# Macaron block (MoE, attention, MoE) on one core: the routing of the second MoE's first half moved later into the last attention batches, with filler products on TensorE

## The reference, cut to what matters

```python
def ffn(x, gate_w, expert_bias, w1, w2, w3):      # 8 experts, top 2, hidden 352
    scores = softmax(x @ gate_w.T)
    _, sel = top_k(scores + expert_bias, 2)
    # token t goes to its two experts, scaled by its score BEFORE the expert
    routed = x[token_idx] * top_scores_sorted[:, None]
    out_rows = (silu(routed @ w1[e]) * (routed @ w3[e])) @ w2[e]   # e by row
    return zeros.at[token_idx].add(out_rows)

def attn(x, Wq, Wk, Wv, Wo):                      # 16 heads of width 8, no mask
    return softmax(q @ k.T / sqrt(8)) @ v @ Wo.T

x = hidden_states                                 # 16 x 256 tokens, width 128
x = x + 0.5 * ffn(layernorm(x), ...)
x = x + attn(layernorm(x), ...)
x = x + 0.5 * ffn(layernorm(x), ...)              # same weights again
```

## Time and profile before

| | us |
|---|---|
| median of 3 runs | 765.34 (761.83 to 770.02) |
| the profiled execution | 765.52 |
| its span | 763.7 |
| start to attention's batch 0 | 254.5 |
| batches 13, 14, 15 with the seam's first part | 469.08 to 529.46 |
| first transpose of the second network's first load | 531.76 |
| last expert product | 712.5 |
| end, result gathers and stores | 763.7 |

### The profile page before, as it was taken

One profiled execution on the slowest core, in us unless ns is written; L12 is line 12 of the kernel. 1 busy time (PEld: TensorE's weight loads), 2 busy tenths in 40 slices (PEclk: granted clock), 3 DMA queues, 4 the chain that ended last, 5 costly groups with the idle time before them and its releaser, 6 DMA issues.

```text
span 763.7 us, 14753 instructions
## 1 busy us (share of the span) xinstructions
PE 623.9 (82%) x4966; PEld 465.6 (61%) x4966; DVE 445.6 (58%) x1163; ACT 389.8 (51%) x910; POOL 303.2 (40%) x313
## 2 busy tenths in 40 slices
PE   5248999999988788889889998888999989999200
PEld 5237898999866334445445554344889979999200
DVE  4845753225454888898999999871567422233111
ACT  0524665444422567767777777575356544444000
POOL 6057533665433226254000010003375137777574
PEclk9999999999999779999999999776999999999655
DMA  7255888877982444535334443034478768887422
GB/s 253 69 182 147 238 245 230 227 230 211 282 245 76 140 129 121 161 112 152 114 98 130 124 135 104 2 98 155 115 197 243 238 185 231 260 243 224 112 79 62
DMA packets 116298, 126.02 MB, mean 165 GB/s; under 512 B 12480, under 2 KB 99008, under 8 KB 115968
## 3 DMA queue, kind: packets, MB, share of 16 engines
q1 hardware_dynamic: 98256, 100.15, 43.6%
q0 software_dynamic: 9088, 18.63, 9.9%
q10 hardware_dynamic: 8880, 6.30, 2.5%
HBM read 89.37 MB, written 35.39 MB: 163 GB/s over the span
## 4 chain that ended last, share of the span: by engine, by line
PE 58%; DVE 20%; DMA 6%; issue 5%; ACT 5%; POOL 5%; SPq 1%; POOLq 0%; ACTq 0%; DVEq 0%
PE banks L673 13%; PE banks L645 9%; PE banks L654 9%; PE banks L661 8%; DVE mx L805 8%; PE banks L1050 6%; POOL rows L580 4%; PE banks L467 3%; ACT PT L1064 2%; PE banks L635 2%; DMA xe<-routed_rows,idx 2%; PE banks L934 2%; PE banks L1023 2%; DMA X<-in_x 1%; DVE resid L792 1%
## 5 line engine op out<-in xcount | busy, mean ns | idle before, releaser
L560 POOL DMA_INDIRECT xe<-routed_rows,idx x156 | 151.8, 973 | 241.5 <-DVE idx L434 105.0
L805 DVE TENSOR_REDUCE mx<-banks 128x2 f32<-128x512 f32 x256 | 163.5, 684 | 9.7 <-PE banks L1025 8.6
L1064 ACT ACTIVATE PT<-banks 128x512 f32<-128x512 f32 x256 | 141.5, 604 | 48.4 <-PE banks L1036 46.2
L580 POOL DMA_INDIRECT rows<-slots_out,slot x128 | 123.3, 963 | 67.4 <-issue 27.8
L726 DVE TENSOR_TENSOR hidT<-banks,act 96x256 f32<-96x256 f32 (+1 forms) x92 | 34.9, 380 | 189.2 <-ACT act L707 188.9
L673 PE MATMUL banks<-WR,hidT 128*128 128x128 f32 x936 | 119.8, 275 | 0.6 <-ACT ye L716 0.6
L673 PEld LDWEIGHTS banks<-WR,hidT 128*128 128x128 f32 x936 | 111.9, 191 | 3.0 <-issue 1.0
L645 PE MATMUL banks<-xeT,WR 128*128 128x256 f32 (+1 forms) x368 | 87.6, 361 | 5.9 <-issue 3.0
L1023 PE MATMUL banks<-KS,QS 56*128 56x256 bf16 x256 | 70.0, 289 | 18.8 <-DVE mx L805 15.1
L654 PE MATMUL banks<-xeT,WR 128*96 128x256 f32 (+1 forms) x368 | 84.4, 352 | 0.0
L661 PE MATMUL banks<-xeT,WR 128*128 128x256 f32 (+1 forms) x368 | 83.3, 349 | 0.0
(11 more groups left out here) (156 smaller groups left out, 865.4 us busy)
## 6 DMA issues: line engine op xcount, KB each, us to landing
WR<-in_experts SPq DMA_DIRECT2D x92, 544.0 KB
stacks<-split SPq DMA_DIRECT2D x32, 384.0 KB
slots_out<-ye SPq DMA_DIRECT2D x156, 64.0 KB
QS<-stacks SPq DMA_DIRECT2D x64, 112.0 KB
KS<-stacks SPq DMA_DIRECT2D x64, 112.0 KB
routed_rows<-xn ACTq DMA_DIRECT2D x16, 256.0 KB, 5.6
routed_rows<-xn SPq DMA_DIRECT2D x12, 256.0 KB, 2.3
xe<-routed_rows,idx POOLq DMA_INDIRECT x156, 4.9
```

Source lines behind the costliest of these rows:

```text
L560: eng.indirect_dma_start(xe[:, i % XR, a, :], None, routed_rows[h], bass.IndirectOffsetOnAxis(ap=idx[h][:, tile:tile + 1], axis=0))\
L580: eng.indirect_dma_start(rows[:, k, t, :], None, slots_out[h], bass.IndirectOffsetOnAxis(ap=slot[h][:, k, t:t + 1], axis=0))\
L805: eng.tensor_reduce(mx[:, :, e, pair], maxima_bank(f)[:, :].rearrange("p (q n) -> p q n", q=2), AX.X, ALU.max).then_inc(s_max, 1)
L1064: eng.activation(PT[:, u % 4, 1 - k].rearrange("p t n -> p (t n)"), PS[f % 3], ACT.Exp, scale=scale).then_inc(s_exp2, 1)
```

## The change

It changes when pieces of routing g = 2 stand in the queues of DVE, ACT, PE and SP; what is computed for the output is the same. In addition PE gets 18 products of constants (`keep_pace`: the identity times WO, 128x128 float32, written to bank 4 of the accumulator memory and never read): one after each step from 118 to 127 and eight in the seam.

```diff
         def last_rows_sync(eng):
-            for k, c in ((1, 0), (1, 1), (0, 0), (1, 2), (1, 3), (0, 1), (0, 2), (0, 3)):
+            for k, c in ((0, 0), (0, 1), (1, 0), (1, 1), (1, 2), (0, 2), (1, 3), (0, 3)):
+                if (k, c) == (1, 2):
+                    weights(eng, HALVES * NL)
+                    weights(eng, HALVES * NL + 1)
...
                     advance(side, ticks, PAIRS * n + u)
+                    if PAIRS * n + u > PAIRS * (BATCH - 2) + 5:
+                        keep_pace(eng, 1)
+
+        def keep_pace(eng, products):
+            for _ in range(products):
+                eng.matmul(PS[4][:, 0:D], ident, WO[:], start=True, stop=True)
...
-            expert_sync(sp, HALVES * NL, 2 * HALVES * NL)
+            expert_sync(sp, HALVES * NL, 2 * HALVES * NL, begun=2)
...
             side = route_scalar(act, 2)
-            attention_scalar(act, side, spans((103, 103, 17), (113, 113, 23), (114, 119, 1), (120, 123, 2), (124, 124, 1)))
+            attention_scalar(act, side, spans((105, 105, 17), (117, 117, 23), (118, 127, 1)))
+            ending = ending_scalar(act)
+            next(ending)
             for _ in side:
                 pass
-            ending = ending_scalar(act)
-            next(ending)
...
-            attention_tensor(pe, side, spans((115, 115, 39), (122, 122, 33), (123, 125, 1)))
+            attention_tensor(pe, side, spans((117, 117, 39), (125, 125, 33), (126, 126, 1)))
+            ending = ending_tensor(pe)
+            next(ending)
             for _ in side:
                 pass
-            ending = ending_tensor(pe)
-            next(ending)
+            keep_pace(pe, 8)
...
-            side = chained(route_norm(dve, 8, 0, 1), route_vector(dve, 2, 0))
+            side, made = chained(route_norm(dve, 8, 0, 1), route_vector(dve, 2, 0)), rows_vector(dve)
...
-                             (side, spans((72, 73, 1), (80, 81, 1), (88, 89, 1), (96, 96, 3), (97, 97, 1), (101, 101, 12),
-                                     (104, 106, 2), (108, 111, 1), (112, 112, 14), (116, 116, 1), (117, 119, 2),
-                                     (120, 120, 3), (121, 121, 2), (122, 123, 1), (124, 124, 2), (126, 126, 18)), None),
-                             (rows_vector(dve), spans((113, 114, 1), (115, 115, 2)), None))
-            for _ in side:
+                             (side, spans((72, 73, 1), (80, 81, 1), (88, 89, 1), (96, 96, 3), (97, 97, 1), (104, 104, 12),
+                                     (106, 107, 1), (109, 109, 1), (111, 113, 1), (114, 114, 2), (115, 115, 3),
+                                     (116, 116, 13), (118, 119, 2), (120, 121, 3), (122, 123, 2), (125, 125, 2)), None),
+                             (made, spans((124, 124, 1), (126, 127, 1)), None))
+            for _ in chained(made, side):
```

More of the change, by code:

```diff
@@ L597, in combine, with weights, expert_sync @@
                 yield
-        def expert_sync(eng, first, last, *sides):
-            lag = 2
-            def weights(i):
-                g, l, w, row = load_of(i)
-                if l == 0:
-                    eng.wait_ge(s_expert, g + 1)
-                e = eng.value_load(expert[g % HALVES][0:1, l:l + 1], min_val=0, max_val=EXPERTS - 1)
-                wait(eng, s_y, i - WRING + 1)
-                eng.dma_start(WR[:, i % WRING, :], experts[bass.ds(e, 1), :, :].squeeze(0))\
-                   .then_inc(s_wl[i % WRING], 16)
+        def weights(eng, i):
+            g, l, w, row = load_of(i)
+            if l == 0:
+                eng.wait_ge(s_expert, g + 1)
+            e = eng.value_load(expert[g % HALVES][0:1, l:l + 1], min_val=0, max_val=EXPERTS - 1)
+            wait(eng, s_y, i - WRING + 1)
+            eng.dma_start(WR[:, i % WRING, :], experts[bass.ds(e, 1), :, :].squeeze(0))\
+               .then_inc(s_wl[i % WRING], 16)
+        def expert_sync(eng, first, last, *sides, begun=0):
+            lag = 2
             def rows_out(i):
@@ L618, in expert_sync @@
             for i in range(first, last + lag + 2):
-                if i < last:
-                    weights(i)
+                if first + begun <= i < last:
+                    weights(eng, i)
                 if i - lag - 2 >= first:
```

## The result

| | before | after |
|---|---|---|
| median of 20 runs each, us | 767.1 (761.83 to 770.5) | 762.47 (758.98 to 766.34) |
| profiled execution, us | 765.52 | 760.37 |
| its span, us | 763.72 | 758.57 |

The ratio after to before is 0.9939 (95% interval 0.9923 to 0.9954): the change makes the kernel 0.6% faster, 4.7 us, which is clear of noise but under the one percent that the prediction calls a change. Busy time in stretches of the changed kernel: batch 13, 14, 15 with the transpose of X, the stage from there to the last expert product, and the one stretch at the lower clock in it (columns as in the earlier trace rows).

What follows compares the result with a forecast made beforehand. DVE was taken to bound most attention batches, and PE, behind the result of the first expert load, the rest. Terms -3.2 - 4.5 - 2.6 + 7.7 + 0.7 = -1.9 from 765.52 gave 763.6 us, range 757 to 770.5.

Steps and rivals of the forecast that it cites:

- Batch 13: Steps 104 to 111: DVE loses eight statistics and two splits, gets nine routing instructions; 14.6 us against 17.78, -3.2.
- Batch 14: Steps 112 to 119: less attention work, more routing, two products of constants at 0.4 together; 14.7 us against 19.24, -4.5.
- Batch 15: To the end of L1001: routing chain through DVE ends 14.0 after step 118 starts; 20.8 us against 23.36, -2.6.
- the wait for `on` in step 125: Batch 15: PE waits about 1.1 us for DVE's normalisation, a new wait.
- Seam: Transpose of X to first load's: four `xn`, last store's landing, then gather; +10.0 us against 2.3, +7.7.
- The estimate from the Trainium skill: Seam: a GpSimd DMA takes 2.15 us for 64 KB, making the seam about 1 us shorter, sum 762.6.
- Clock into the experts: After the idle seam, the lower clock level lasts longer in the expert stage; +0.7 us, ends 0 and +3.4.
- Moved weights gain nothing: Fetching weights 46 and 47 ahead gains nothing: PE waited for gathers, not for them.
- the low gather price: Seam: 5.33 us from last store landed to first transpose, since only two weight transfers still stand behind that store.
- Rival 1: Seam: weights 48 and 49 slow last row store and gathers; seam 13.5 or more, sum 767.1; chance 0.17.
- Rival 2: Steps 115 to 126 at the lower clock despite products; batches 14 and 15 take 17.5 and 24.5, 770.1; chance 0.2.
- Rival 3: Batches 13, 14, 15 at 14.0, 14.0, 19.4, seam 9.0, no more lower clock: 759.2; chance 0.14.

Runs made afterwards that it cites:

- top2_back: Changed kernel with softmax and top 2 of routing g = 2 back in steps 101 to 111 on DVE, its exponential after step 103 on ACT; 766.45 us, ratio 0.9999.
- no_products: Changed kernel without any of the 18 products of constants; 765.54 us, ratio 0.9986.
- weights_last: Changed kernel with the weights of the first two expert loads fetched behind all row stores again; 766.05 us, ratio 0.9994.
- weights_held: rearranged, but first load's weights right behind the last store, later ones only after the first load's gathers landed; 20 products in the seam; 753.83 us, ratio 0.985.
- all_in_steps: Changed kernel with the last four `xn`, last eight one-hot products and all DVE `rows` in the steps instead of the seam; 761.81 us, ratio 0.9939.
- rearranged: Changed kernel with one-hot products, `xn` and DVE `rows` moved into steps, stores in the order they come free, two weight transfers before the last four; 762.35 us, ratio 0.9942.
- before_products: Kernel before with one product of constants after each of steps 118 to 127, nothing moved; 770.13 us, ratio 1.0053.

## Why the prediction was right, point by point

The forecast was 763.6 us from an execution of 765.52, -1.9; that execution's like came out at 760.37, -5.15, and the median at 762.47, inside the range. That 763.6 lies so near the median is in part luck: over 20 runs the kernel before takes 767.1, not 765.34, so a forecast change of -1.9 stands against a measured 0.6% or -4.7. The mechanism was the forecast's, no rival's, but its size was less than half. In the profiles the miss of 3.25 us is made of: the three terms of gain, all sized too small (1.18); the start of batch 13, which the change does not touch (0.46); what follows the first load, -1.46 where +0.7 was forecast (2.16); less the seam, 0.55 longer than forecast.

- **Batch 13, -3.2 forecast, -3.79.** Right, and shown by top2_back: putting the instructions back costs 4.32 there. The batch took 13.99 for 14.6: seven routing instructions stood in it where I counted nine (0.6 us at 0.31 each), and the two small normalisations that drop out are worth 0.67 where I took 0.2; that is somewhat more than the miss.
- **Batch 14, -4.5, -4.61.** Right in size; no_products shows 14.41 without the two products, so they cost 0.22, half of the 0.4 that I took.
- **Batch 15, -2.6, -3.08.** Right as a chain: the wait for `on` in step 125 was forecast at 1.1 and measured 0.98. There is a slip in the sum, though: 11.8 and 1.8 are 13.6, not 14.0, and measured from the start of step 118 to the end of the last one-hot half it is 13.70. Whether five of the eight products cost nothing there, as forecast, no run shows, since without them the clock falls.
- **Seam, +7.7, +8.25.** Right: four `xn` behind `xrT`, then store, landing, gather. From landing to first transpose 5.27 for 5.33. The mis-sized term is the store: 3.16 us, where I had 2.3. The weights moved ahead are what held it up: behind the same three stores and no weights it took 2.40 (weights_last). ACT made up 0.24 of it (+2.11 for +2.35). The estimate from the Trainium skill, page DMA: Bandwidth & Descriptors, section on the anatomy of one DMA, by which this chain was to be about 1 us shorter, is not borne out: a gather took 3.03 here against the estimated 2.15. In weights_held, with little else on the engines (DMA share 0.21 while it ran), it took 2.50.
- **Clock into the experts, +0.7.** The low time from the first load on was 4.9 us for 3.4, which cost 0.4 by the end of the first load's down products. The rest of the stage came out 1.8 shorter through gaps that the sum had at nothing (the fourth routing's first load, -1.15).
- **"Moved weights gain nothing" was wrong.** It is the step of the prediction that failed. I asked whether PE waits for weights 46 and 47, and it does not; but a transfer that nobody waits for still stands ahead of the gathers on the DMA engines, and without that part of the change the seam is 2.3 us longer and the kernel about 4 us slower (weights_last). My own paragraph on the seam gave the two transfers fetched ahead as the reason for the low gather price, so the price was in the sum but credited to no part of the change.
- **Rival 1** (store held up by weights) did not decide this change: 5.49 was not reached. But it was at work, by 0.76 us, and since the three stores before it were late as well, mainly from the transfers ahead of them and not the two behind that I named; it is what all_in_steps and rearranged run into at 6.00 and 6.30. It bounds the seam as soon as the stores are early.
- **Rival 2** (the products do not hold the clock) fell for batch 15 of this change: without them it is 4.46 us longer, near the 3.7 priced. They are no guarantee: four of the other kernels that have them fall to the lower level for 3.4 us in step 125 or 126, and before_products does for 6.8 us. Its evidence, a busy PE at the lower level, was right in itself: no_products has 19.85 busy of 20.48 us at 0.50. What I set against it was wrong in one of three cases: the fall at 512.50 in the kernel before followed a wait of 1.18 us for ACT (L1064), not for DVE. By the page TensorE: Matmul & The Clock Gate of the Trainium skill, section What's actually happening, the throttled clock is the default and activity releases it; the busy time of PE alone does not bear that out here, with 19.85 of 20.48 us in no_products and, products among them, 6.82 of 6.82 in before_products.
- **Rival 3** was priced at 759.2 and needed a cheap seam; the profiled 760.37 is nearer to it than to the forecast, by way of the batches and not of the seam.

## What to carry to other kernels

Ask of a prefetch not only who waits for its data but who queues behind its bytes: holding back weight transfers until the small gathers had landed, with twelve more products beside it, was worth about 7 us where the whole change was worth 4.7. Take instructions out of the engine whose result the next step waits for, and put them where that engine itself waits; then look at the clock, since a fall behind a wait of about 1 us cost up to 4.5 us here. Filler products paid in batch 15 of the change, where the waits beside them had become thin, and not in the kernel before, where the clock fell all the same.

## What the runs showed of the hardware that was not expected

- The lower clock followed waits of PE of only about 1 us: 1.22 before, 1.23 in top2_back, 0.80 and 0.66 in no_products, and in four of eight kernels the wait of step 125 (0.98 in the changed one, 1.00 in these). Such a wait does not decide it: the other four kept the clock behind the same wait, and three of 0.66 to 0.88 us stand in batch 14 of all eleven kernels that have batches 13 and 14 as changed, at 1.00 throughout. Once down, the clock stayed there for 3.4 to 20.5 us, in top2_back and no_products with PE busy 89 and 97% of the time.
- A gather of 64 KB took 2.50 us with one weight transfer issued 3.1 us ahead of it, 3.03 with two issued in the 3.8 us ahead of it, 6.09 with four, the first issued 3.1 us ahead and the last just after. A store of 256 KB took 2.28 with little beside it (DMA share 0.44), 3.16 where two weight transfers had gone ahead of its three forerunners, 2.40 without these, and 6.30 in rearranged, behind two transfers and three stores and ahead of two more transfers.
- The profiled executions reach the start of batch 13 between 467.9 and 471.9 us, though the programs up to there are the same but for a few instructions. Executions of one kernel spread as much (758.98 to 766.34 us for the changed one), so this need not be a difference between the kernels; and 4 us is as much as most of the effects here, so the batches' own lengths (batch 13 takes 13.98 to 14.00 in all eleven kernels that have it as changed) tell more than a span does.
